# Extra products in TensorE's waits, and a later place for the stores of keys and values, in a cross-attention and coupling kernel

## The chip, the cores and the metric

The kernel runs on one core of a Trainium2 chip. The metric is the device time of one execution in microseconds (us). TensorE multiplies matrices (PE in the profile, PEld its weight loads), VectorE is DVE, ScalarE is ACT, GpSimd is POOL, and SyncE (SP) issues the DMAs.

## The reference

```python
x = x + xattn(layernorm(x), ctx)            # x 8 x 1024 x 512, ctx 8 x 64 x 512, 16 heads of 32
x = x + ffn(layernorm(x))

def xattn(q, kv):
    qh, kh = phase_sync(heads(q @ Wq.T + bq)), phase_sync(heads(kv @ Wk.T + bk))
    a = softmax(qh @ kh.T / sqrt(32))
    return merge(a @ heads(kv @ Wv.T + bv)) @ Wo.T + bo

def ffn(x):
    gf = global_net(x.mean(over the 1024 rows))          # three small layers
    out = x
    for _ in range(3):                                   # three cycles
        tf = sigmoid(gelu(gelu(gelu(out @ w1 + b1) @ w2 + b2) @ w3 + b3) @ w4 + b4)
        out = out + (0.1 + arange * (0.7 * gf + 0.3 * tf - 0.5) * 2) * twist(out)
    return out
```

## The kernel before

Each engine has one program, an ordered list of steps written out by hand, and semaphores between them. An engine never goes past a step whose wait is not over. There are eight batches of 1024 rows, each in two blocks (k) of 512 rows, and each block in four tiles of 128 rows (j or t). The attention of batch b runs interleaved with the coupling network of batch p = b - 1.

**Attention.** ScalarE normalizes a tile into PSUM and rounds it to f16 (`xh`, L764), VectorE makes the low half (`xl`, L1827), and SyncE issues a DMA transpose (`x_turn`, L3079) into `xoT`, or `x2T` for the second normalization. `xr` has two buffers, so `xh` of a tile waits until the transpose of the tile two before it has landed. `q` (L286) are 12 products of the query weights, `s` (L304) the scores of one tile (24 products into two PSUM banks), VectorE takes the maximum (L1839) and subtracts it (`sub`, L1847), ScalarE takes the exponential (L792), GpSimd normalizes, the probabilities are split (L804, L1869) and turned by DMA (`p_turn`, L3092). `pv` (L320) multiplies by the values, ScalarE and VectorE drain it (L815, L1874), and `wo` (L335, L337) is the output product of one tile, 13 products, drained by VectorE (L1881).

**Coupling network.** A batch has four units of 256 rows (k, h), dealt to three lanes of buffers, with a fourth lane for the last unit of all. `y` (L387) are 24 products of 256 columns into a lane's PSUM bank, drained by ScalarE (L837). `gz` (L344) are the global net's products; they wait for the column sums `gsum` (ScalarE, L776) of the whole batch. Each of three cycles of a unit goes `act1` (ScalarE, L850), rounding (VectorE, L1918) and low half (GpSimd, L2851), `l2` (L402, twice 12 products), `act2` (L858), `l3` (L414), `act3` (L866), `l4` (L422), and the coupling back on ScalarE (L877, L885), VectorE and GpSimd.

**Setup.** The keys and values of all batches are computed at the start into `kst` and `vst`. `kv_load(0)` takes batch 0's from there. `kv_store` (L3010, L3014) writes all of them to DRAM, and `kv_load(b)` of later batches reads them back from there; it and the first `y` of each lane wait for `kv_stored`. `load_next` (L3025) loads the next batch's x.

TensorE's bank numbers: `BANK_X` 0, scores `BANK_S` 1 and 2, `BANK_M` 3 and 4, lanes `BANK_F` 5, 6, 7 and 3.

Of the kernel before, what the change touches and what calls it, by code (L numbers as in the profile page):

```python
# [15 lines left out]
B, S, D = 8, 1024, 512  # L16
# [26 lines left out]
def cols(j):  # L43
    return slice(j * P, (j + 1) * P)


def program(nc, x, ctxT, wq, bq, wk, bk, wvT, bv, woT, bo, phase, cw1, cb1, cw2, cb2, cw3, cb3, cw4, cb4,
# [5 lines left out]
    with ExitStack() as ctx:  # L53
# [164 lines left out]
        def tensor_program(e):  # L218
# [53 lines left out]

            @staged
# [132 lines left out]
            @staged  # L406
            def l3(p, k, h, cy):
                L, u = unit(p, k, h)
                i = 3 * u + cy
                e.wait_ge(lg[L]["g2"], base(L, "g2") + 2 * i + 2)  # L410
                if u + cy == 0:
                    e.wait_ge(loaded["w3"], 16)
                for c in range(C2):
                    mm = e.matmul(ps[:, BANK_F[L], 0:LBLK], W3[:, c], zb[L][:, c], start=(c == 0), stop=(c == C2 - 1))  # L414
                mm.then_inc(lg[L]["l3"], 1)
# [17 lines left out]
            s(0, 0); s(0, 1); s(0, 2)  # L433
# [3 lines left out]
            s(0, 4); s(0, 5); s(0, 6)  # L437
            pv(0, 0, 0); pv(0, 0, 1)
            s(0, 7)
            wo(0, 0); wo(0, 1); wo(0, 2); wo(0, 3)  # L440
            pv(0, 1, 0); pv(0, 1, 1)
            wo(0, 4); wo(0, 5); wo(0, 6); wo(0, 7)
            y(0, 0, 1, 0); y(0, 0, 0, 0); y(0, 0, 1, 1); y(0, 1, 0, 0); y(0, 0, 1, 2); y(0, 1, 0, 1)
# [75 lines left out]
            for b, p in zip(range(2, 7), range(1, 6)):  # L519
# [60 lines left out]
                l2(p, 1, 1, 1, 0); l2(p, 1, 1, 1, 1)  # L580
                l3(p, 1, 1, 1)
                l4(p, 1, 1, 1)
# [65 lines left out]
            l2(6, 1, 1, 1, 0); l2(6, 1, 1, 1, 1)  # L648
            l3(6, 1, 1, 1)
            l4(6, 1, 1, 1)  # L650
# [35 lines left out]
            l2(7, 1, 0, 1, 0); l2(7, 1, 1, 0, 0); l2(7, 1, 1, 0, 1)  # L686
            l3(7, 1, 1, 0)
            l4(7, 1, 1, 0)
            l2(7, 1, 0, 1, 1)
            l3(7, 1, 0, 1)  # L690
            l4(7, 1, 0, 1)
            l2(7, 1, 1, 1, 0); l2(7, 1, 1, 1, 1)
            l3(7, 1, 1, 1)
            l4(7, 1, 1, 1)
            l2(7, 0, 1, 2, 0); l2(7, 0, 1, 2, 1); l2(7, 1, 0, 2, 0)
            l3(7, 0, 1, 2)
            l2(7, 1, 0, 2, 1)
            l4(7, 0, 1, 2)
            l3(7, 1, 0, 2)
            l4(7, 1, 0, 2)  # L700
            l2(7, 1, 1, 2, 0); l2(7, 1, 1, 2, 1)
            l3(7, 1, 1, 2)
            l4(7, 1, 1, 2)
# [2292 lines left out]
        def sync_program(e):  # L2996
# [140 lines left out]
            kv_store(0)  # L3137
# [4 lines left out]
            p_turn(0, 6, 0); p_turn(0, 7, 0); p_turn(0, 6, 1); p_turn(0, 7, 1)  # L3142
            load_next(0, 0)
# [158 lines left out]
```

## Time and profile before

| | |
|---|---|
| median of 3 runs | 1371.53 us (1369.87 to 1373.86) |
| the profiled execution's own time | 1371.05 us |
| its span, first to last instruction | 1369.0 us |
| mean granted TensorE clock over the span | 0.964 |
| PE busy | 1244.9 us (91%) |
| DVE, ACT, POOL busy | 1053.6, 1052.0 and 614.5 us |

The granted clock is the share of TensorE's full clock that it was given: 1.00 is 2.4 GHz, 0.50 is 1.2 GHz. The profile's own page cuts the span into 40 slices of 34.2 us.

### The profile page before, as it was taken

To read this page: it belongs to the slowest core of one execution; us is meant where nothing else is said; L and a number is where in the kernel's file an instruction comes from. 1 tells how busy PE (TensorE), PEld (TensorE's weight loads), DVE (VectorE), ACT (ScalarE), POOL (GpSimd) and SP (SyncE) were. 2 spreads that over 40 slices of the span, in tenths; PEclk is the share of its full clock that TensorE was granted. 3 is DMA by queue.
4 is the path that set the end of the run, shared out by engine and by line. 5 is a ranking of instruction groups with operands and counts; after the bars stand their busy time and mean duration, and the time that the engine had idled before them with its cause. 6 is when DMAs were issued, how large, how long until landed. Compare 5 with 4: busy or idle time off the path is not lost.

```text
span 1369.0 us, 27539 instructions
## 1 busy us (share of the span) xinstructions
PE 1244.9 (91%) x10264; PEld 868.0 (63%) x10264; DVE 1053.6 (77%) x2097; ACT 1052.0 (77%) x1886; POOL 614.5 (45%) x488
## 2 busy tenths in 40 slices
PE   7756899989999999999999999999999999988974
PEld 5322665658666776658666776658666776657863
DVE  4787459995889769985899669995899669994565
ACT  3444768888887978888887978888887877877655
POOL 0032025572455526562455526562455526462563
PEclk9967999999999999999999999999999999999997
DMA  7554423434254345433354335433354334431001
GB/s 246 156 88 108 91 49 72 93 70 98 53 119 80 71 78 93 102 71 93 71 108 79 77 71 93 102 70 93 72 107 78 81 75 78 78 52 42 32 1 62
DMA packets 323156, 114.81 MB, mean 84 GB/s; under 512 B 302416, under 2 KB 309456, under 8 KB 320848
## 3 DMA queue, kind: packets, MB, share of 16 engines
q1 hardware_dynamic: 323024, 113.06, 39.2%
q8 instruction: 81, 1.33, 0.4%
q14 instruction: 51, 0.42, 0.1%
HBM read 26.66 MB, written 18.87 MB: 33 GB/s over the span
## 4 chain that ended last, share of the span: by engine, by line
PE 60%; ACT 15%; DVE 11%; issue 6%; DMA 3%; POOL 2%; SPq 1%; ACTq 0%; DVEq 0%; POOLq 0%
PE ps L387 19%; PE ps L402 11%; PE ps L286 11%; PE ps L335 7%; ACT spent L776 4%; PE ps L414 3%; PE ps L304 2%; PE ps L422 2%; ACT z L850 2%; DMA x2T<-xr 2%; ACT z L858 2%; DVE xr L1827 2%; DVE z L1939 1%; DVE z L1927 1%; ACT xoT L815 1%
## 5 line engine op out<-in xcount | busy, mean ns | idle before, releaser
L2851 POOL TENSOR_TENSOR h<-z,h 128x512 f16<-128x512 f32 x186 | 234.6, 1271 | 385.5 <-DVE h L1918 385.5
L387 PE MATMUL ps<-x2T,W 128*128 128x256 f16 x3072 | 351.1, 273 | 6.6 <-ACT Y L837 4.0
L387 PEld LDWEIGHTS ps<-x2T,W 128*128 128x128 f16 x3072 | 297.4, 98 | 56.9 <-issue 8.8
L402 PE MATMUL ps<-h,W 128*128 128x256 f16 x2232 | 273.0, 280 | 6.4 <-POOL h L2851 6.2
L402 PEld LDWEIGHTS ps<-h,W 128*128 128x128 f16 x2232 | 221.7, 101 | 54.5 <-issue 13.7
L2844 POOL TENSOR_TENSOR prob<-prob,rc 128x512 f32<-128x512 f32 x128 | 140.1, 1117 | 104.2 <-DVE rc L1863 104.2
L335 PE MATMUL ps<-WO,xoT 128*128 128x512 f16 x768 | 180.1, 385 | 5.0 <-DVE xoT L1874 5.0
L286 PE MATMUL ps<-xoT,WQ 128*128 128x512 f16 x768 | 174.3, 380 | 0.7 <-issue 0.5
L1827 DVE TENSOR_TENSOR xr<-ps,xr 128x512 f16<-128x512 f32 x128 | 87.8, 686 | 82.9 <-ACT xr L764 82.6
L2860 POOL TENSOR_TENSOR z<-Y,coup 128x512 f32<-128x512 f32 x62 | 100.2, 1616 | 83.5 <-ACT coup L885 69.7
L850 ACT ACTIVATE z<-z,b_col 128x256 f32<-128x256 f32 x248 | 113.2, 500 | 30.7 <-DVE z L1939 30.6
L335 PEld LDWEIGHTS ps<-WO,xoT 128*128 128x128 f16 x768 | 75.4, 99 | 91.2 <-issue 7.2
L1918 DVE CAST h<-z 128x512 f16<-128x512 f32 x186 | 96.3, 531 | 46.4 <-ACT z L850 46.0
L286 PEld LDWEIGHTS ps<-xoT,WQ 128*128 128x128 f16 x768 | 74.5, 98 | 87.9 <-issue 4.6
L414 PE MATMUL ps<-z,W 128*128 128x256 f32 x372 | 100.7, 397 | 22.6 <-ACT z L858 21.8
L858 ACT ACTIVATE z<-ps,b_col 128x256 f32<-128x256 f32 x186 | 79.9, 470 | 49.1 <-PE ps L402 49.0
L2867 POOL TENSOR_TENSOR Y<-Y,coup 128x512 f32<-128x512 f32 x62 | 92.3, 1506 | 23.4 <-DVE coup L1951 23.4
L1939 DVE TENSOR_TENSOR z<-z,Y 128x512 f32<-128x512 f32 x124 | 97.4, 797 | 6.7 <-POOL Y L2867 4.9
L837 ACT ACTIVATE Y<-ps 128x512 f32<-128x512 f32 x124 | 71.6, 590 | 35.6 <-PE ps L387 35.3
L2837 POOL TENSOR_TENSOR rs<-ve,minus_half 128x4 f32<-128x4 f32 x32 | 35.6, 1113 | 131.0 <-DVE ve L1815 130.9
L414 PEld LDWEIGHTS ps<-z,W 128*128 128x128 f32 x372 | 65.5, 191 | 42.9 <-ACT z L858 32.7
L1839 DVE TENSOR_REDUCE mx<-ps 128x8 f32<-128x512 f32 x128 | 81.8, 673 | 12.1 <-PE ps L304 11.8
(159 smaller groups left out, 2064.2 us busy)
## 6 DMA issues: line engine op xcount, KB each, us to landing
xin<-x SPq DMA_DIRECT2D x16, 1024.0 KB, 5.5
out<-ot SPq DMA_DIRECT2D x64, 256.0 KB, 2.5
factor_rows<-coup SPq DMA_DIRECT2D x186, 0.5 KB, 2.1
pT<-pr SPq DMA_TRANSPOSE x128, 3.2
wq_s<-wq SPq DMA_DIRECT2D x1, 1024.0 KB, 5.9
wk_s<-wk SPq DMA_DIRECT2D x1, 1024.0 KB, 10.4
ctx_s<-ctxT SPq DMA_DIRECT2D x4, 256.0 KB, 10.3
wv_s<-wvT SPq DMA_DIRECT2D x1, 1024.0 KB, 10.9
```

The source lines that it names most:

```text
L286: mm = e.matmul(ps[:, bank], w, v, start=(n == 0), stop=(n == 3 * C - 1))
L335: e.matmul(ps[:, BANK_M + i % 2], w, v, start=(n == 0), stop=False)
L387: mm = e.matmul(ps[:, BANK_F[L], at * LBLK:(at + 1) * LBLK], w, v, start=(n == 0), stop=(n == 3 * C - 1))
L402: mm = e.matmul(ps[:, BANK_F[L], m * LBLK:(m + 1) * LBLK], w, v, start=(c + m + a == 0), stop=(c == C - 1 and m == C2 - 1 and a == 2))
L414: mm = e.matmul(ps[:, BANK_F[L], 0:LBLK], W3[:, c], zb[L][:, c], start=(c == 0), stop=(c == C2 - 1))
L850: e.activation(z[L][:, m], src, ACT.Gelu, bias=b1_col[:, m:m + 1]).then_inc(lg[L]["g1"], 1)
L858: e.activation(zb[L][:, m], src, ACT.Gelu, bias=b2_col[:, m:m + 1], scale=1.0 / WSCALE).then_inc(lg[L]["g2"], 1)
L1827: e.tensor_tensor(xr[:, n % 2, LO], ps[:, BANK_X], xr[:, n % 2, HI], ALU.subtract).then_inc(sg["xl"], 1)
L1939: e.tensor_tensor(z[L][:, pair(n)], z[L][:, pair(n)], Y[L][:, pair(n), 0], ALU.add).then_inc(lg[L]["pre"], 1)
L2844: e.tensor_tensor(part, part, wide(half_heads(rc[:, j], g)), ALU.mult).then_inc(sg["nrm"], 1)
L2851: e.tensor_tensor(h1[L][:, LO, pair(n)], z[L][:, pair(n)], h1[L][:, HI, pair(n)], ALU.subtract).then_inc(lg[L]["lo1"], 1)
L2860: e.tensor_tensor(z[L][:, pair(1)], Y[L][:, pair(1), 1], wide2(c1[L] if cy == 1 else b2[L]), ALU.mult).then_inc(lg[L]["mulg"], 1)
```

## The change

A helper `weight_products` issues n products of a part of the query weights with another part. Nothing reads their results. In batch 0 they go into lane 0's PSUM bank (`in_lane_bank`, once lane 2's), 512 columns each, 95 of them in twelve places. In each pass of batches p = 1 to 5 they go into the upper half of a lane's bank (`beside`), 256 columns each, 10 ahead of `l3(p, 1, 1, 1)` and 3 ahead of the `l4` behind it; in pass 6 it is 14 and 3. In the last batch they go into a score bank (`in_score_bank`), 512 columns each, 36 in fourteen places. Each group waits for a semaphore that frees its bank. `kv_store` moves from behind `x_turn(0, 0, 1, 0)` to behind the last `p_turn` of batch 0.

```diff
--- before.py
+++ after.py
@@ -270,6 +270,23 @@
                                   start=(c == 0), stop=(c == C - 1))
                 mm.then_inc(su["v_mul"], 1)
 
+            def weight_products(at, n):
+                for _ in range(n):
+                    e.matmul(at, WQ[:, HI, 0, cols(0)], WQ[:, HI, 1, 0:at.shape[-1]], start=True, stop=True)
+
+            def in_lane_bank(L, n):
+                e.wait_ge(su["v_lo"], B // 2)
+                weight_products(ps[:, BANK_F[L]], n)
+
+            def in_score_bank(n):
+                e.wait_ge(sg["sub"], 16 * B)
+                weight_products(ps[:, BANK_S], n)
+
+            def beside(p, k, h, cy, n):
+                L, u = unit(p, k, h)
+                e.wait_ge(lg[L]["g2"], base(L, "g2") + 2 * (3 * u + cy) + 2)
+                weight_products(ps[:, BANK_F[L], LBLK:BLK], n)
+
             @staged
             def q(b, k, m):
                 i = 24 * b + 4 * k + m
@@ -430,17 +447,36 @@
             q(0, 0, 0)
             vmul(0, 1); vmul(0, 2); vmul(0, 3)
             q(0, 0, 1); q(0, 0, 2); q(0, 0, 3)
-            s(0, 0); s(0, 1); s(0, 2)
+            in_lane_bank(0, 5)
+            s(0, 0)
+            in_lane_bank(0, 9)
+            s(0, 1)
+            in_lane_bank(0, 6)
+            s(0, 2)
             q(0, 1, 0)
             s(0, 3)
             q(0, 1, 1); q(0, 1, 2); q(0, 1, 3)
-            s(0, 4); s(0, 5); s(0, 6)
-            pv(0, 0, 0); pv(0, 0, 1)
+            in_lane_bank(0, 5)
+            s(0, 4)
+            in_lane_bank(0, 14)
+            s(0, 5)
+            in_lane_bank(0, 9)
+            s(0, 6)
+            pv(0, 0, 0)
+            in_lane_bank(0, 13)
+            pv(0, 0, 1)
             s(0, 7)
+            in_lane_bank(0, 8)
             wo(0, 0); wo(0, 1); wo(0, 2); wo(0, 3)
-            pv(0, 1, 0); pv(0, 1, 1)
+            in_lane_bank(0, 2)
+            pv(0, 1, 0)
+            in_lane_bank(0, 8)
+            pv(0, 1, 1)
+            in_lane_bank(0, 8)
             wo(0, 4); wo(0, 5); wo(0, 6); wo(0, 7)
-            y(0, 0, 1, 0); y(0, 0, 0, 0); y(0, 0, 1, 1); y(0, 1, 0, 0); y(0, 0, 1, 2); y(0, 1, 0, 1)
+            y(0, 0, 1, 0); y(0, 0, 0, 0)
+            in_lane_bank(2, 8)
+            y(0, 0, 1, 1); y(0, 1, 0, 0); y(0, 0, 1, 2); y(0, 1, 0, 1)
             gz(0, 0)
             y(0, 0, 0, 1); y(0, 1, 0, 2)
             gz(0, 1)
@@ -578,7 +614,9 @@
                 l4(p, 1, 0, 1)
                 wo(b, 6); wo(b, 7)
                 l2(p, 1, 1, 1, 0); l2(p, 1, 1, 1, 1)
+                beside(p, 1, 0, 1, 10)
                 l3(p, 1, 1, 1)
+                beside(p, 1, 0, 1, 3)
                 l4(p, 1, 1, 1)
                 l2(p, 0, 1, 2, 0); l2(p, 0, 1, 2, 1); l2(p, 1, 0, 2, 0); l2(p, 1, 0, 2, 1)
                 l3(p, 0, 1, 2); l3(p, 1, 0, 2)
@@ -646,7 +684,9 @@
             l4(6, 1, 0, 1)
             wo(7, 6); wo(7, 7)
             l2(6, 1, 1, 1, 0); l2(6, 1, 1, 1, 1)
+            beside(6, 1, 0, 1, 14)
             l3(6, 1, 1, 1)
+            beside(6, 1, 0, 1, 3)
             l4(6, 1, 1, 1)
             l2(6, 0, 1, 2, 0); l2(6, 0, 1, 2, 1); l2(6, 1, 0, 2, 0); l2(6, 1, 0, 2, 1)
             l3(6, 0, 1, 2); l3(6, 1, 0, 2)
@@ -684,22 +724,37 @@
             y(7, 1, 1, 3)
             l4(7, 0, 1, 1)
             l2(7, 1, 0, 1, 0); l2(7, 1, 1, 0, 0); l2(7, 1, 1, 0, 1)
+            in_score_bank(3)
             l3(7, 1, 1, 0)
+            in_score_bank(1)
             l4(7, 1, 1, 0)
             l2(7, 1, 0, 1, 1)
+            in_score_bank(3)
             l3(7, 1, 0, 1)
+            in_score_bank(3)
             l4(7, 1, 0, 1)
+            in_score_bank(5)
             l2(7, 1, 1, 1, 0); l2(7, 1, 1, 1, 1)
+            in_score_bank(3)
             l3(7, 1, 1, 1)
+            in_score_bank(1)
             l4(7, 1, 1, 1)
-            l2(7, 0, 1, 2, 0); l2(7, 0, 1, 2, 1); l2(7, 1, 0, 2, 0)
+            in_score_bank(2)
+            l2(7, 0, 1, 2, 0)
+            in_score_bank(2)
+            l2(7, 0, 1, 2, 1); l2(7, 1, 0, 2, 0)
             l3(7, 0, 1, 2)
             l2(7, 1, 0, 2, 1)
             l4(7, 0, 1, 2)
+            in_score_bank(6)
             l3(7, 1, 0, 2)
+            in_score_bank(1)
             l4(7, 1, 0, 2)
+            in_score_bank(2)
             l2(7, 1, 1, 2, 0); l2(7, 1, 1, 2, 1)
+            in_score_bank(3)
             l3(7, 1, 1, 2)
+            in_score_bank(1)
             l4(7, 1, 1, 2)
 
         def scalar_program(e):
@@ -3134,12 +3189,12 @@
             load_late(0, 0); load_late(0, 2); load_late(0, 3); load_late(0, 1)
             kv_load(0)
             x_turn(0, 0, 1, 0)
-            kv_store(0)
             x_turn(0, 0, 1, 1); x_turn(0, 0, 1, 2); x_turn(0, 0, 1, 3)
             load_late(0, 4)
             p_turn(0, 0, 0); p_turn(0, 1, 0); p_turn(0, 0, 1); p_turn(0, 1, 1); p_turn(0, 2, 0); p_turn(0, 2, 1)
             p_turn(0, 3, 0); p_turn(0, 3, 1); p_turn(0, 4, 0); p_turn(0, 4, 1); p_turn(0, 5, 0); p_turn(0, 5, 1)
             p_turn(0, 6, 0); p_turn(0, 7, 0); p_turn(0, 6, 1); p_turn(0, 7, 1)
+            kv_store(0)
             load_next(0, 0)
             x_turn(0, 1, 0, 0); x_turn(0, 1, 0, 1); x_turn(0, 1, 0, 2); x_turn(0, 1, 0, 3)
             kv_load(1)
```

TensorE's order where batch 0's scores begin. Before (L286 is `q`, L304 `s`, L320 `pv`):

```order
L286 MATMUL ps<-xoT,WQ 128x512 x36
L304 MATMUL ps<-kblocks,qT 128x128 x72
L286 MATMUL ps<-xoT,WQ 128x512 x12
L304 MATMUL ps<-kblocks,qT 128x128 x24
L286 MATMUL ps<-xoT,WQ 128x512 x36
L304 MATMUL ps<-kblocks,qT 128x128 x72
L320 MATMUL ps<-pT,vblocks 32x512 x48
L304 MATMUL ps<-kblocks,qT 128x128 x24
```

The changed kernel has the same steps (L303 is `q`, L321 `s`), and L275 are the extra products; `ps<-WQ` is all that they name:

```order
L303 MATMUL ps<-xoT,WQ 128x512 x36
L275 MATMUL ps<-WQ 128x512 x5
L321 MATMUL ps<-kblocks,qT 128x128 x24
L275 MATMUL ps<-WQ 128x512 x9
L321 MATMUL ps<-kblocks,qT 128x128 x24
L275 MATMUL ps<-WQ 128x512 x6
L321 MATMUL ps<-kblocks,qT 128x128 x24
L303 MATMUL ps<-xoT,WQ 128x512 x12
L321 MATMUL ps<-kblocks,qT 128x128 x24
L303 MATMUL ps<-xoT,WQ 128x512 x36
L275 MATMUL ps<-WQ 128x512 x5
L321 MATMUL ps<-kblocks,qT 128x128 x24
```

The 72 products of three tiles of scores, which stood together, now have 9 and 6 extra products between them and 5 ahead, and so on in the next three.

SyncE's order in batch 0, from the loads of keys and values. Before (L3010 and L3014 are `kv_store`, L3079 `x_turn`, L3092 `p_turn`, L3025 `load_next`):

```order
L3042 DMA kblocks<-kst 32x2x256 x4
L3079 DMA_TRANSPOSE xoT<-xr 128x8x128
L3010 DMA k_blocks<-kst 128x4096
L3014 DMA v_blocks<-vst 64x8x256 x4
L3079 DMA_TRANSPOSE xoT<-xr 128x8x128 x3
L3001 DMA b_col<-cb 128x4
L3001 DMA b_col<-cb 128x2
L3001 DMA b_col<-cb 128x1
L3001 DMA gb_col<-gb 128x2
L3001 DMA gb_col<-gb 128x1
L3092 DMA_TRANSPOSE pT<-pr 128x8x128 x16
L3025 DMA xin<-x 128x2048
```

After (L3134 is `x_turn`, L3147 `p_turn`, L3065 and L3069 `kv_store`, L3080 `load_next`):

```order
L3097 DMA kblocks<-kst 32x2x256 x4
L3134 DMA_TRANSPOSE xoT<-xr 128x8x128 x4
L3056 DMA b_col<-cb 128x4
L3056 DMA b_col<-cb 128x2
L3056 DMA b_col<-cb 128x1
L3056 DMA gb_col<-gb 128x2
L3056 DMA gb_col<-gb 128x1
L3147 DMA_TRANSPOSE pT<-pr 128x8x128 x16
L3065 DMA k_blocks<-kst 128x4096
L3069 DMA v_blocks<-vst 64x8x256 x4
L3080 DMA xin<-x 128x2048
L3134 DMA_TRANSPOSE x2T<-xr 128x8x128 x4
```

The five stores went past three transposes of x, five small loads and 16 transposes of probabilities. They now stand ahead of the next batch's load and of the four transposes into `x2T`.

TensorE's order at the end of a pass (p = 2). Before (L402 is `l2`, L414 `l3`, L422 `l4`):

```order
L402 MATMUL ps<-h,W 128x256 x24
L414 MATMUL ps<-z,W 128x256 x2
L422 MATMUL ps<-z,W 128x256
L402 MATMUL ps<-h,W 128x256 x48
L414 MATMUL ps<-z,W 128x256 x4
```

After (L419 is `l2`, L431 `l3`, L439 `l4`; the trace shows twice as many records for the f32 products as stand here):

```order
L419 MATMUL ps<-h,W 128x256 x24
L275 MATMUL ps<-WQ 128x256 x10
L431 MATMUL ps<-z,W 128x256 x2
L275 MATMUL ps<-WQ 128x256 x3
L439 MATMUL ps<-z,W 128x256
L419 MATMUL ps<-h,W 128x256 x48
L431 MATMUL ps<-z,W 128x256 x4
```

The 10 and the 3 extra products stand ahead of `l3` and ahead of `l4`; the 48 products of four `l2` behind them did not move.

## Rows read from the trace of the kernel before

**Rows 1.** The page: granted clock by slice, and the ending chain by engine.

```profile
PEclk9967999999999999999999999999999999999997
...
PE 60%; ACT 15%; DVE 11%; issue 6%; DMA 3%; POOL 2%; SPq 1%; ACTq 0%; DVEq 0%; POOLq 0%
```

**Rows 2.** Busy time by stretch, then granted clock, DMA share, GB/s.

```profile
60.00:145.00 85.00, 52.22 (x442) 24.88 (x443) 63.21 (x104) 35.55 (x46) 19.15 (x17) 0.76 0.55 115
...
449.97:456.80 6.83, 6.16 (x27) 4.18 (x27) 5.63 (x9) 6.40 (x13) 6.11 (x6) 0.50 0.20 39
```

**Rows 3.** The chain that ended last, 56 to 160 us: start, length.

```profile
66.30 5.45 DMA xoT<-xr
...
95.14 1.48 PE ps L304 x24
...
105.81 1.53 PE ps L320 x18
...
110.94 4.23 PE ps L335 x12
...
131.28 5.05 PE ps L335 x12
```

**Rows 4.** The timeline, 60 to 73 us: start, length, [idle <-releaser].

```profile
60.66 5.54 SPq L3014 DMA_DIRECT2D v_blocks<-vst  x4
...
64.90 1.29 DVE L1839 TENSOR_REDUCE mx<-ps 128x8 f32<-128x512 f32 x2 [0.27 <-PE ps L304]
...
72.46 0.69 DVE L1827 TENSOR_TENSOR xr<-ps,xr 128x512 f16<-128x512 f32 x1 [6.27 <-ACT xr L764]
```

**Rows 5.** DMA issues, 38 to 140 us: count, median us to landing.

```profile
x2T<-xr SPq DMA_TRANSPOSE x4, 3.1
```

**Rows 6.** TensorE's waits, 58 to 155 us: total, times, longest.

```profile
PE ps L304 <- DVE prob L1847: 18.6, 4, 9.5
PE ps L320 <- DVE xoT L1874: 6.2, 2, 3.8
PE ps L335 <- DVE xoT L1874: 4.5, 2, 2.3
PE ps L304 <- DVE qT L1832: 3.4, 2, 1.7
PE ps L387 <- ACT Y L837: 2.2, 1, 2.2
```

**Rows 7.** The timeline, TensorE's groups while the granted clock was 1.00.

```profile
90.38 0.84 PE L304 MATMUL ps<-kblocks,qT 64*128 64x128 f16 x24 [1.71 <-DVE qT L1832]
...
121.04 2.75 PE L335 MATMUL ps<-WO,xoT 128*128 128x512 f16 x12
...
128.18 0.84 PE L320 MATMUL ps<-pT,vblocks 64*32 64x512 f16 x24 [2.45 <-DVE xoT L1874]
...
444.23 2.78 PE L402 MATMUL ps<-h,W 128*128 128x256 f16 x24
```

**Rows 8.** The timeline of ScalarE, 142 to 160 us.

```profile
142.33 1.06 ACT L776 ACTIVATE spent<-x2T 128x1024 f16<-128x1024 f16 x1 [3.92 <-DMA x2T<-xr]
...
148.22 0.78 ACT L755 ACTIVATE ps<-xin,nm,rs 128x512 f32<-128x512 f32 x1 [1.19 <-DVE nm L1821]
...
159.52 0.60 ACT L837 ACTIVATE Y<-ps 128x512 f32<-128x512 f32 x1 [0.81 <-PE ps L387]
```

**Rows 9.** The timeline, 448 to 461 us: TensorE, VectorE and ScalarE.

```profile
448.89 1.13 PE L414 MATMUL ps<-z,W 128*128 128x256 f32 x4 [1.87 <-ACT z L858]
...
451.70 7.89 PE L402 MATMUL ps<-h,W 128*128 128x256 f16 x48
...
458.38 0.67 DVE L1827 TENSOR_TENSOR xr<-ps,xr 128x512 f16<-128x512 f32 x1
...
459.63 0.84 ACT L858 ACTIVATE z<-ps,b_col 128x256 f32<-128x256 f32 x2 [1.78 <-PE ps L402]
```

**Rows 10.** The timeline of TensorE in the last products.

```profile
1348.53 4.01 PE L402 MATMUL ps<-pT,W 128*128 128x256 f16 x24 [0.64 <-POOL pT L2851]
```

## The prediction

> **What bounds the kernel now.** I read the page first. The chain that ended last lies on PE for 60%, and the granted clock is full in all but the third and fourth slice and, slightly, at the ends [rows 1]. So TensorE is the bound from about 145 us on, and the start is something else. The stretches say what: from 60 to 145 us PE is busy for 52 of 85 us at a mean clock of 0.76, while VectorE is busy for 63 [rows 2]. The chain there passes from engine to engine, and where it is on PE its pieces are long: a `wo` of 12 products takes 4.23 and 5.05 us [rows 3], where the same 12 take 2.75 at full clock [rows 7]. In each later pass one low stretch is left, as 449.97 to 456.80 us at exactly 0.50 [rows 2]. It falls behind a wait of 1.87 us ahead of `l3`, and holds most of the 48 products of four `l2`, which take 7.89 us [rows 9] against twice 2.78 for 24 at full clock [rows 7].
>
> **The stores, moved.** SP issues the five stores ahead of the transpose of the sixth tile; the four of the values alone occupy it for 5.54 us [rows 4], and that transpose then takes 5.45 us from issue to landing among their data [rows 3]. Such transposes take 3.1 us in the median elsewhere in this stretch [rows 5]. ScalarE cannot round the eighth tile until that landing, VectorE waits for ScalarE, and behind this wait in VectorE's order stand the subtraction of the second tile of scores and all that follows. Without the stores the transpose is issued at about 60.1, where the stores began, and lands by 63.3. The next thing VectorE is late for is its own maximum, which ends at 66.19 (64.90 + 1.29), and the step that began at 72.46 can follow at once: its idle time was 6.27 us [rows 4]. I take **-6.3**. The next tile's transpose leaves earlier by the same amount, so TensorE's second `q` does too.
>
> What the stores cost in the new place: they go out behind the last transpose of probabilities, with nothing to wait for, and SP has about 9 us before the first transpose into `x2T` is ready; their issue takes some 6 and the load of x behind them less than 1. So the issue is hidden. The data are not quite: 2 MB of stores and 1 MB of x are in flight when that transpose goes. Right behind the stores a transpose took 5.45 instead of 3.1 us, which bounds the price at 2.3; zero is the other end. ScalarE has no slack there, since it waited 3.92 us for the last of these transposes [rows 8]. The last store is about 4 us old instead of new, so I take **+1.5**.
>
> **The extra products in batch 0.** 12 products of 512 columns take 2.75 us at full clock [rows 7], 0.23 each. 93 of the 95 lie in waits that sum to 34.9 us [rows 6], of which 6.3 go with the stores: 28.6 us of waiting against 21.4 of products. The largest group but one, 13, takes 3.0 us in a wait of 3.8 [rows 6]. At full clock each group ends before its wait does, so they cost nothing; what hides them is VectorE's softmax.
>
> Their effect is that TensorE's idle stretches shrink to under 1 us in most places, so the clock that the profile shows at 0.50 for most of this stretch should stay at 1.00. On the chain this is worth, up to the first normalization of the second kind: scores 1.48 to 0.84, **-0.6**; `pv` 1.53 to 0.84 or 0.89, **-0.6**; the first `wo` 4.23 to 2.75, **-1.4** [rows 3, 7]. The rest of the chain is VectorE's and does not change. With the stores that makes 8.9. The second group of `wo`, 5.05 to 2.75, would give 2.3 more, but the transposes into `x2T`, on which ScalarE's column sums wait, start ahead of it and move by 8.9 only. ScalarE then goes from the sums to the next normalization, where it had 1.19 us of slack [rows 8]; so I count **-1.2** of the 2.3. The `y` products after the eighth group of 8 also ran partly at 0.50; ScalarE was idle for them for 0.81 us [rows 8], so **-0.8**. Start: -6.3 - 2.6 - 1.2 - 0.8 + 1.5 = **-9.4**.
>
> **The passes.** 24 products of 256 columns take 2.78 us [rows 7], 0.116 each: 10 take 1.2 us of the 1.87 us wait, 3 take 0.35 us ahead of `l4`. They cost nothing while ScalarE is busy with the column sums, which it is for all of that wait. If the clock stays up, the 48 `l2` products need 5.6 instead of 7.9 us. But not all 2.3 us are passed on. ScalarE waited only 1.78 us for them, and the normalization right behind its `act2` needs VectorE's low half, which ends at 459.05 (458.38 + 0.67) [rows 9], where it began at about 460.4 (behind 459.63 + 0.84). This limits the gain to **-1.3** for a pass; what is late next is VectorE, with its coupling work. The transposes, the sums and `gz` behind it all move by 1.3, and from there TensorE is the bound again. Five passes show this low stretch at the same place, each of 6.8 us: **-6.5**. In the sixth (pass 6) the low stretch is 3.4 us, and the chain there runs over a transpose of 5.1 us, so I count nothing.
>
> **The last batch.** 36 products of 0.23 us stand in waits of 0.6 to 1.8 us, in groups of 1 to 6; they fit. Two low stretches lie there. Only the last one is on the chain: 24 products in 4.01 us [rows 10] against 2.78, **-1.2**. The other delays a unit whose result waits in ScalarE's order anyway.
>
> **The sum.** Against the profiled execution's 1371.05 us, which is 0.5 below the median: 1371.05 - 9.4 - 6.5 - 1.2 = 1353.95, so 1354.
>
> **Rivals.**
> *The clock falls all the same* (0.19). Products of 64 rows or 32 columns, f32 products and waits of 0.3 to 1 us stay between the extra ones, and a pass that is shorter by 1 us puts its waits at another moment each time, as it does to the longer waits of batch 1's start, behind which nothing fell before. Then the passes give nothing: 1371.05 - 10.6 = 1360.
> The Trainium skill ("TensorE: Matmul & The Clock Gate", A second HAM failure mode) says that frequent micro-idles between groups of products make the clock oscillate; by that rule the products bring little where short waits remain, and the time would be this 1360. The trace agrees only in part: from 300 to 1150 us it shows many short waits and a fall at one of them alone in each pass.
>
> *The stores collide with the transposes* (0.08). If the transposes into `x2T` queue behind all of the stores' and the load's data, each of the first two is late by up to 2.3 us and the loss of the start is given back: the gain of 6.3 shrinks to about 0, 1371.05 - 17.1 + 6.3 = 1360.
>
> *More is passed on* (0.10). VectorE's order behind the passes' `l2` is not as rigid as I read it, all 2.3 us pass, and the stores cost nothing: 1354 - 5 x 1.0 - 1.5 = 1347.5.
>
> *The extra products overrun* (0.03), the case on the other side. Should the clock stay at 0.50 in batch 0, as it did for much of it, a product takes 5.05 / 12 = 0.42 us [rows 3], and 93 take 39 us in 28.6 us of waits: at least 10.4 us are added to the chain. In the passes 10 take 2.1 us in 1.87, some 0.3 for each, and in the last batch about 3 more. With the stores' 4.8 gained: 1371.05 + 10.4 + 1.5 + 3 - 4.8 = 1381. It decides once more than about half of batch 0's groups run at the low clock. The profile speaks against it: where PE is busy without a break the clock comes back, in the passes after 6.83 us [rows 2], and the first groups start while it is still at 1.00.
>
> **How the numbers follow.** My forecast has 0.60: 1349 to 1359, with the collision's bounds (0 to 2.3) and 0.5 to 1.5 for each pass. With the first two rivals at 1360 the range has to reach up, with the third down: 1346 to 1363. It leaves out the overrun and mixtures of the first two. A measurement of this kernel tells 0.3%, 4.1 us, from no change. Faster is every case but the overrun and a coincidence of clock and collision: 0.93; within 0.3% 0.04; slower 0.03.
>
> **What would show it.** VectorE's idle of 6.27 us at the eighth tile gone, and the second `q` 6 us earlier; granted clock near 1.00 from 60 to 145 us, with `wo` groups of 2.75; `y` of batch 0 beginning some 9 to 10 us earlier; passes of about 152.4 us from `l3` to `l3` instead of 153.8, with 48 `l2` products in under 6; the last 24 in 2.8. I would be wrong if `x2T`'s transposes land late, if `l3` or `l4` starts behind an extra product instead of behind ScalarE, or if the low stretch only moves.

## The result, and the profile after

The changed kernel takes 1366.18 us (median of 7 runs, 1363.12 to 1369.19); the kernel before, run beside it, 1371.53 (7 runs, 1368.99 to 1374.48). The ratio is 0.996 with a 95% interval of 0.9944 to 0.9975: faster, by 5.35 us, where 17 were forecast. The time lies outside the range. The profiled execution took 1366.63 us against 1371.05, 4.4 less; that is the difference which the traces can be asked about.

The page of the kernel after: TensorE's busy time, its granted clock by slice, and the chain that ended last, by engine.

```profile
PE 1267.1 (93%) x10477; PEld 877.7 (64%) x10477; DVE 1051.8 (77%) x2097; ACT 1050.1 (77%) x1886; POOL 614.6 (45%) x488
...
PEclk9989999999999999999999999999999999999998
...
PE 57%; ACT 16%; DVE 14%; issue 7%; DMA 3%; POOL 3%; SPq 1%; ACTq 0%; DVEq 0%; POOLq 0%
```

The 6 and the 7 of [rows 1] are gone, and the mean clock rose from 0.964 to 0.989. Read by the clock alone the change did what it should. The stretches of [rows 2], asked again (busy time by stretch, then granted clock, DMA share, GB/s):

```profile
60.00:145.00 85.00, 68.06 (x535) 30.94 (x534) 65.00 (x106) 37.00 (x49) 19.14 (x17) 0.94 0.62 115
...
450.00:457.00 7.00, 5.94 (x41) 4.26 (x42) 5.88 (x8) 6.60 (x15) 6.64 (x6) 1.00 0.20 37
```

So the time is to be looked for elsewhere. I set the same group of TensorE against itself in both traces, and noted by how much it comes earlier:

| place on TensorE | before, us | after, us | earlier by |
|---|---|---|---|
| second `q`, (0,1,0) | 76.37 | 71.55 | 4.8 |
| first `wo` starts | 110.94 | 106.60 | 4.3 |
| first `wo` ends | 115.17 | 109.35 | 5.8 |
| first transpose into `x2T` issued (SP) | 132.41 | 127.61 | 4.8 |
| `gz(0)` | 166.25 | 164.77 | 1.5 |
| `gz(1)`, pass 0 between them | 315.99 | 318.40 | -2.4 |
| `gz(7)`, passes 1 to 6 between them | 1245.29 | 1241.78 | 3.5 |
| end of the span | 1369.0 | 1364.6 | 4.4 |

Four sums stand in it: the start gave 1.5 us (forecast 9.4), pass 0 took 3.9 (forecast nothing), passes 1 to 6 gave 5.9 (forecast 6.5), the last batch 0.9 (forecast 1.2). A pass is here the way from `gz(0)` of one batch to that of the next.

**Where the start went.** TensorE's waits from 58 to 155 us, as in [rows 6]: what is waited for, total, times, longest.

```profile
PE ps L321 <- DVE prob L1902: 4.9, 4, 3.0
PE ps L352 <- DVE xin L1936: 4.5, 2, 4.3
PE ps L337 <- DVE xoT L1929: 2.6, 2, 2.1
PE ps L352 <- DVE xoT L1929: 1.8, 2, 1.4
PE ps L337 <- DMA pT<-pr: 1.4, 1, 1.4
```

The waits for `prob` and `xoT` shrank, filled by products and shortened by the stores' departure. Two are new: `wo` waits 4.3 us for VectorE's `xin`, and `pv` 1.4 us for a transpose of probabilities. SP's timeline there: start, length.

```profile
118.29 0.53 SPq L3065 DMA_DIRECT2D k_blocks<-kst  x1
118.87 5.67 SPq L3069 DMA_DIRECT2D v_blocks<-vst  x4
124.58 1.31 SPq L3080 DMA_DIRECT2D xin<-x  x1
```

And the chain of the same stretch: start, length, what.

```profile
116.17 3.94 DMA pT<-pr
...
120.19 0.89 PE ps L337 x24
...
127.61 6.87 DMA x2T<-xr
...
134.56 0.61 ACT xr L819
...
135.19 0.69 DVE xr L1882
135.88 0.61 DVE xin L1936
...
136.53 4.45 PE ps L352 x12
```

The transpose issued at 127.61, 3.0 us behind the issue of the load, lands after 6.87 us; [rows 5] have 3.1. ScalarE needs its landing to overwrite `xr`, VectorE's low half stands behind ScalarE, `xin` stands behind that in VectorE's order, and the third `wo` needs `xin`. TensorE is idle for 4.27 us, the granted clock falls to 0.50 (from 137.4 to 140.8 us), and 12 products take 4.45 us, not 2.75.

**The passes.** The stretch of [rows 9] in the kernel after, TensorE: start, length, count, [idle before it].

```profile
448.15 1.26 PE L275 MATMUL ps<-WQ 128*128 128x256 f16 x10
450.17 1.13 PE L431 MATMUL ps<-z,W 128*128 128x256 f32 x4 [0.76 <-ACT z L913]
451.13 0.49 PE L275 MATMUL ps<-WQ 128*128 128x256 f16 x3
...
452.96 3.04 PE L419 MATMUL ps<-h,W 128*128 128x256 f16 x24 [0.30 <-POOL h L2906]
456.16 2.78 PE L419 MATMUL ps<-h,W 128*128 128x256 f16 x24 [0.16 <-POOL h L2906]
```

`l3` still starts behind ScalarE, not behind an extra product; the 48 products take 5.8 us, not 7.89, and no low stretch is left in passes 1 to 6. In pass 0, which has no extra products, two have appeared that the kernel before did not show. The first of them, in the kernel before and, below the dots, in the kernel after:

```profile
227.18 1.13 PE L414 MATMUL ps<-z,W 128*128 128x256 f32 x4 [1.74 <-ACT z L858]
228.88 0.70 PE L422 MATMUL ps<-z,W 128*128 128x256 f32 x2 [0.57 <-ACT z L866]
229.41 1.03 PE L414 MATMUL ps<-z,W 128*128 128x256 f32 x4
...
227.97 1.13 PE L431 MATMUL ps<-z,W 128*128 128x256 f32 x4 [1.73 <-ACT z L913]
229.67 1.22 PE L439 MATMUL ps<-z,W 128*128 128x256 f32 x2 [0.56 <-ACT z L921]
230.68 1.91 PE L431 MATMUL ps<-z,W 128*128 128x256 f32 x4
```

The second group of four f32 products takes 1.03 us before and 1.91 after: the clock stood at 0.66 in the mean from 229 to 234 us, and it fell again from 297.8 to 301.2. The wait ahead of the first group is the same in both, 1.74 and 1.73 us; only behind the second of them does the clock fall.

### The profile page after: what moved, and what is told of

The parts are those of the page before. It is cut to its first block, busy times and chain, and to the rows that moved or that the text cites. A ratio compares the mean times of both kernels' runs of the same rounds, so it can differ in the third digit from the quotient of the medians.

```text
span 1364.6 us, 27965 instructions
## 1 busy us (share of the span) xinstructions
PE 1267.1 (93%) x10477; PEld 877.7 (64%) x10477; DVE 1051.8 (77%) x2097; ACT 1050.1 (77%) x1886; POOL 614.6 (45%) x488
## 4 chain that ended last, share of the span: by engine, by line
PE 57%; ACT 16%; DVE 14%; issue 7%; DMA 3%; POOL 3%; SPq 1%; ACTq 0%; DVEq 0%; POOLq 0%
PE ps L404 19%; PE ps L303 12%; PE ps L419 9%; PE ps L352 6%; ACT spent L831 4%; PE ps L431 3%; PE ps L321 2%; DVE xr L1882 2%; DMA x2T<-xr 2%; ACT xr L819 2%; ACT z L905 2%; ACT ps L810 2%; PE ps L439 2%; DVE z L1994 1%; ACT z L913 1%
## 5 line engine op out<-in xcount | busy, mean ns | idle before, releaser
L404 PEld LDWEIGHTS ps<-x2T,W 128*128 128x128 f16 x3072 | 296.2, 98 | 55.9 <-issue 9.9
L419 PE MATMUL ps<-h,W 128*128 128x256 f16 x2232 | 265.8, 274 | 9.0 <-POOL h L2906 8.1
L419 PEld LDWEIGHTS ps<-h,W 128*128 128x128 f16 x2232 | 215.8, 98 | 55.4 <-issue 19.7
L303 PE MATMUL ps<-xoT,WQ 128*128 128x512 f16 x768 | 175.5, 382 | 4.7 <-issue 4.6
L303 PEld LDWEIGHTS ps<-xoT,WQ 128*128 128x128 f16 x768 | 74.7, 98 | 93.1 <-issue 10.8
L431 PE MATMUL ps<-z,W 128*128 128x256 f32 x372 | 99.0, 394 | 13.6 <-ACT z L913 12.6
L1894 DVE TENSOR_REDUCE mx<-ps 128x8 f32<-128x512 f32 x128 | 81.9, 673 | 15.6 <-PE ps L321 15.3
L431 PEld LDWEIGHTS ps<-z,W 128*128 128x128 f32 x372 | 65.8, 191 | 33.9 <-ACT z L913 23.4
```

The costliest lines, as they stand in the source:

```text
L303: mm = e.matmul(ps[:, bank], w, v, start=(n == 0), stop=(n == 3 * C - 1))
L404: mm = e.matmul(ps[:, BANK_F[L], at * LBLK:(at + 1) * LBLK], w, v, start=(n == 0), stop=(n == 3 * C - 1))
L419: mm = e.matmul(ps[:, BANK_F[L], m * LBLK:(m + 1) * LBLK], w, v, start=(c + m + a == 0), stop=(c == C - 1 and m == C2 - 1 and a == 2))
```

## The experiments

Each ran beside the kernel before on its own chip, and the ratio is to that; medians of different chips are compared by their ratios only. "Alone" means on the kernel before. My theory ahead of them: the stores' new place makes the transposes into `x2T` late, and this, with what follows in pass 0, is where the gain went. The main rival: the clock falls somewhere else as soon as one fall is filled, so that products in general bring little.

**1. The stores in the change's place, alone** (`e1_store_alone`).

```diff
             x_turn(0, 0, 1, 0)
-            kv_store(0)
...
             p_turn(0, 6, 0); p_turn(0, 7, 0); p_turn(0, 6, 1); p_turn(0, 7, 1)
+            kv_store(0)
```

> The kernel before with the five stores moved to their new place and no extra product. Theory A (the stores collide with the transposes into x2T in the new place): VectorE's wait of 6.3 us at the eighth tile is gone, some 5 us are gained by 80 us, and one of the four first transposes into x2T takes over 5 us and gives 2 to 4 us of it back; the sums' product gz of batch 0 stands 1 to 3 us earlier than before, time 1368 to 1371. Theory B (the extra products, not the stores, ate the gain): all four transposes land in 3 to 4 us, gz stands 5 to 6 us earlier, time 1365 to 1366.5.

Measured: 1369.37 us against 1373.29, ratio 0.9971 (0.9948 to 0.9993). It gained 4.9 us at the third tile of scores (69.54 against 74.40) and kept 2.3 of them at `gz(0)` (164.00). The first transpose into `x2T` left 5.4 us behind the load here and took 4.66 us. The numbers are those of theory A, but the loss is not where it puts it: of the 2.6 us, 2.4 are gone before that transpose is issued (129.91 against 132.41), because the second `q` took 4.76 us at the low clock instead of 3.49, and the first `wo` 5.28 instead of 4.23. The way from that issue to `gz(0)` is only 0.25 us longer than before (34.09 against 33.84): without the products the late landing cost next to nothing.

**2. All products of the change, stores in the old place** (`e2_products_alone`): the change without the piece of experiment 1.

> The changed kernel with the stores back at their old place, so the extra products alone. Theory A: the transposes into x2T take 3.1 us again; the first wo groups run in 2.75 us, gz of batch 0 stands 3 to 5 us earlier than in the kernel before, the passes are as in the changed kernel, time 1362 to 1366, no slower than the changed kernel. Theory B: gz of batch 0 no earlier than before or later, time 1369 to 1373.

Measured: 1367.48 us, ratio 0.9964 (0.9946 to 0.9982). The transposes into `x2T` are on time (3.12 us), TensorE waits for `xin` at most 0.5 us ahead of a `wo`, and the groups of `wo` take 2.76. Yet the first transpose into `x2T` is issued at 132.07, only 0.3 us earlier than before, and `gz(0)` comes 2.2 earlier.

**3. The stores ahead of the transposes of probabilities** (`e3_store_ahead_of_p_turns`), the rest as in the change.

```diff
             load_late(0, 4)
+            kv_store(0)
             p_turn(0, 0, 0); p_turn(0, 1, 0); p_turn(0, 0, 1); p_turn(0, 1, 1); p_turn(0, 2, 0); p_turn(0, 2, 1)
...
-            kv_store(0)
             load_next(0, 0)
```

> The changed kernel with the five stores behind the small loads and ahead of the 16 transposes of probabilities, at about 72 us, where the DMA engines are little used. Theory A: the transposes into x2T take 3.1 us, VectorE no longer waits 5.4 us at 135 us, gz of batch 0 5 to 6 us earlier than in the changed kernel (less 1 to 2 if the first p_turns are late), time 1360 to 1363. Theory B: no more than 1 us from the changed kernel's 1366.

Measured: 1361.55 us, ratio 0.9919 (0.9895 to 0.9942), which just clears the change's 0.9944 to 0.9975. `gz(0)` at 158.39 instead of 164.77. The stores are issued from 71.97 to 77.84, where no transpose is due, and the chain has

```profile
126.38 3.11 DMA x2T<-xr
```

But pass 0 took 155.51 us, with three low stretches (160.6 to 164.0, 222.0 to 228.8, 293.7 to 297.1).

**4. The change without its 82 products in the passes** (`e4_no_pass_products`): the four `beside` calls taken out.

> The changed kernel without the 82 products in the passes p = 1 to 6. If they are worth 1.3 us in each of five passes, as forecast, the distance from gz of batch 1 to gz of batch 7 grows by 6 to 7 us against the changed kernel and the time is 1371 to 1373. If they are worth nothing (the low stretch only moved), both are as in the changed kernel.

Measured: 1379.29 us, ratio 1.0057 (1.0037 to 1.0076): slower than the kernel before by 0.6%. Its profiled run is its fastest (1370.29) and has low stretches in four passes (2, 3, 5 and 6); the other runs show mean clocks of 0.976 to 0.983, where the profiled one has 0.987. From `gz(1)` to `gz(7)` it takes 933.3 us, 9.9 more than the kernel after, where 6 to 7 were expected, and 4.0 more than the kernel before. The low clock is not all of it: pass 4 has no low stretch and takes 155.98 us against 152.97, with two waits on "issue", of 1.80 and 0.85 us, that the kernel after does not have there. For the start this kernel is a repetition of the changed one, with the same code up to there. Its stores are issued from 115.20, and the chain again has

```profile
124.42 6.32 DMA x2T<-xr
```

**5. The 82 products alone** (`e6_pass_products_alone`).

> The kernel before with the 82 products of the passes p = 1 to 6 and nothing else. If a pass gains the forecast 1.3 us by the clock, the five passes are 152.4 us long and the time is 1365 to 1367, 6 to 7 under the kernel before. If the 13 us by which the kernel without them was slower than the changed one are their worth wherever they stand, it is 1359 to 1361. If their worth comes only with the changed start (by the moment at which the clock is decided), it is 1370 to 1373.

Measured: 1368.39 us, ratio 0.9968 (0.9951 to 0.9985), 4 to 5 us, which lies between the expectations of 1365 to 1367 and 1370 to 1373. Passes 1 to 6 sum to 925.5 us against 929.3.

**6. Products in pass 0 too** (`e5_pass0_products`): experiment 3 with 33 more, which leave out nothing and whose result nobody reads. `in_scores(b, n)` is `in_score_bank(n)` with a wait for batch b.

```diff
+            in_scores(1, 6)
             gz(0, 0)
+            in_scores(1, 2)
             y(0, 0, 0, 1); y(0, 1, 0, 2)
             gz(0, 1)
...
+            beside(0, 0, 0, 1, 12)
             l3(0, 1, 0, 0)
+            beside(0, 0, 0, 1, 3)
             l4(0, 1, 0, 0)
...
+            beside(0, 1, 0, 1, 7)
             l3(0, 1, 1, 1)
+            beside(0, 1, 0, 1, 3)
             l4(0, 1, 1, 1)
```

> The stores ahead of the p_turns, as in e3, and 33 more extra products where the clock fell in pass 0 of e3: 6 ahead of the first gz and 2 behind it, 12 and 3 ahead of l3 and l4 of unit (0, 1, 0, 0), 7 and 3 ahead of l3 and l4 of unit (0, 1, 1, 1). Theory C (falls behind waits that stayed unfilled take back part of the start's gain): no stretch at 0.50 between 150 and 300 us, from gz of batch 0 to gz of batch 1 150 to 152 us instead of 155.5, time 1357 to 1360. Against it (these falls are hidden by other engines): the distance stays at 154 or more and the time within 1 us of e3's.

Measured: 1359.03 us, ratio 0.9906 (0.9881 to 0.9931). Pass 0 fell from 155.51 to 152.2 us. TensorE at the `l3` whose wait was 1.73 us in the kernel after:

```profile
218.72 1.48 PE L275 MATMUL ps<-WQ 128*128 128x256 f16 x12
220.53 1.13 PE L435 MATMUL ps<-z,W 128*128 128x256 f32 x4 [0.33 <-ACT z L923]
221.50 0.49 PE L275 MATMUL ps<-WQ 128*128 128x256 f16 x3
222.23 0.70 PE L443 MATMUL ps<-z,W 128*128 128x256 f32 x2 [0.24 <-ACT z L931]
222.76 1.03 PE L435 MATMUL ps<-z,W 128*128 128x256 f32 x4
```

Where experiment 3 and the change show 1.9 us for the second group of `l3`, it is 1.03 here. Two cautions. The ratio is not to be told from experiment 3's. And experiment 8, the same code as experiment 3 up to the last batch, shows 1.03 at this place too, behind its unfilled wait of 1.73 us, and takes 153.73 us for pass 0: the gain of the fillings there is 1.5 to 3.3 us, by which trace it is set against. One low stretch is left in pass 0, from 300.5 to 303.9 us.

**7. Experiment 3 without the 95 products of batch 0** (`e7_no_batch0_products`).

> The changed kernel with the stores ahead of the p_turns (e3) and without the 95 products of batch 0. By the forecast's terms these were worth 0.6 + 0.6 + 1.4 us up to the first normalization of the second kind and 1 to 2 us behind it: gz of batch 0 stands 3 to 5 us later than in e3 and the time is 1364 to 1367. If VectorE hides the slow products, gz stands within 1 us of e3's and the time within 1.5 us.

Measured: 1362.40 us, ratio 0.993 (0.9903 to 0.9957), not to be told from experiment 3. `gz(0)` is 4.1 us later (162.52), pass 0 is 4.3 shorter (151.25), and `gz(1)` is the same (313.77 against 313.90). In these two traces pass 0 takes back all that the products gave in batch 0. In experiment 8, with experiment 3's code up to there, `gz(1)` comes at 312.23, and 1.5 us are left.

**8. Experiment 3 without the 36 products of the last batch** (`e8_no_last_products`).

> The changed kernel with the stores ahead of the p_turns (e3) and without the 36 products of the last batch. By the forecast's term they are worth 1.2 us: 24 products in 4.0 instead of 2.8 us at the end, time 1362 to 1364. Rival: they are worth nothing, or cost, since the groups of 5 and 6 end behind their waits: time 1360 to 1362.

Measured: 1362.94 us, ratio 0.9941 (0.9916 to 0.9965). From `gz(7)` to the end it takes 121.67 us, and experiment 3 takes 121.67 as well: in the trace these products are worth nothing, and the medians don't resolve it.

**9. The stores in the better place, alone** (`e9_store_ahead_alone`): the kernel before with experiment 3's move, no product added.

> The kernel before with one change: the five stores go out on SP behind the last early load of weights and ahead of the transposes of probabilities, instead of ahead of the transpose of the sixth tile. No product is added. My theory (the new place costs only because the transposes into x2T land late behind the stores; the move ahead of the probabilities' transposes keeps the early gain without that cost): gz(0) comes 6 to 7 us earlier than in the kernel before (it was 2.3 earlier with the stores in the place of the change), and the median is 4 to 7 us below the kernel before: 1365 to 1368. Rival (the extra products are what makes the better place pay, since a wait that ends earlier is filled by products at the low clock): gz(0) only 3 to 4 us earlier and the median 2 to 4 us below, 1369 to 1371.

Measured: 1365.40 us against 1372.19, ratio 0.9958 (0.9937 to 0.998). One moved line gives 6.8 us, as much as the whole change. `gz(0)` came 5.9 earlier, just under the 6 to 7 expected.

**10. Seven products more near 297 us** (`e10_gap_at_297`), on experiment 6.

```diff
-            l3(0, 0, 1, 2); l3(0, 1, 0, 2)
+            l3(0, 0, 1, 2)
+            beside(0, 1, 1, 1, 7)
+            l3(0, 1, 0, 2)
```

> The best version so far (stores ahead of the probabilities' transposes, all products of the change, 33 more in pass 0) with 7 more products of 256 columns between l3(0,0,1,2) and l3(0,1,0,2), where its trace shows TensorE idle for 2.89 us behind a transpose that took 4.76 us, and the clock fall behind it. Theory (each fall of the clock follows a single wait that nothing fills): no low stretch at 297 to 304 and pass 1 about 153 us instead of 155.7, median 1 to 3 us below that version. Rival (the late transpose is what cost the pass, and it falls elsewhere in another build): pass 1 near 153 whether or not a low stretch stands there, and the median within 1 us of that version, 1358 to 1360.

Measured: 1358.86 us, ratio 0.9903 (0.9873 to 0.9934), the fastest here and not to be told from experiment 6. The wait stayed, less the time of the products in it, and the low stretch that followed it is gone:

```profile
296.94 0.93 PE L275 MATMUL ps<-WQ 128*128 128x256 f16 x7
299.76 1.13 PE L435 MATMUL ps<-z,W 128*128 128x256 f32 x4 [1.89 <-ACT z L925]
301.02 0.70 PE L443 MATMUL ps<-z,W 128*128 128x256 f32 x2
```

In experiment 6 that wait was 2.89 us, and the four products of `l4` behind it took 2.08; here they take twice 0.70. Pass 1 is 153.07 us, against 155.66. This is not shown to come from the filling: `gz(1)` is no earlier than in experiment 6 (311.41 against 311.05), and the low stretch there ended at 303.9, ahead of it. In experiment 11 the wait at this place was 1.01 us without a filling, no low stretch followed, and pass 1 took 154.27.

**11. Experiment 6 without the 82 products of the passes** (`e11_e5_without_passes`), which asks experiment 4's question again.

> The same best version without the 82 products ahead of l3 and l4 of passes 1 to 6; those of pass 0, of batch 0 and of the last batch stay. It asks again what the pass products are worth: alone on the kernel before they gave 4.8 us, and taking them from the changed kernel cost 13. Theory A (they are worth the filled waits, about 1 us for each of six passes): median 5 to 7 us above that version, 1364 to 1366, with the low stretches of the kernel before back at l3 of most passes. Theory B (together with the other products they are worth more, since a fall in one pass moves others into place): 10 us or more, 1369 and up.

Measured: 1361.42 us, ratio 0.9922 (0.9898 to 0.9946), 2.6 us above experiment 10 on the same chip; passes 1 to 6 sum to 926.3 us against 922.6. Experiment 10 has the seven products near 297 us besides; against experiment 6, from which nothing else differs, the ratios are 2.2 us apart with overlapping intervals, and passes 1 to 6 sum to the same (926.3 and 926.6), since pass 1 ran long there. The low stretches are back in passes 3, 4, 5 and 6. Theory B is out, and A was too high: 2.2 to 2.6 us by the medians, nothing to 3.7 by the traces.

## Why the prediction was wrong

The kernels side by side. The third column is the way from the first transpose into `x2T` to `gz(0)`, which leaves out what happened ahead of it; the last is how long the granted clock stood at 0.50 in pass 0.

| kernel | `x2T` issued | to `gz(0)` | pass 0 | at 0.50 in pass 0 |
|---|---|---|---|---|
| before | 132.41 | 33.84 | 149.74 | 0 |
| 9, stores better, no products | 125.89 | 34.43 | 151.06 | 6.8 |
| 7, the same for the start | 128.68 | 33.84 | 151.25 | 3.4 |
| 1, stores as in the change, no products | 129.91 | 34.09 | 153.78 | 6.8 |
| 2, products, stores not moved | 132.07 | 32.03 | 153.62 | 3.4 |
| after | 127.61 | 37.16 | 153.63 | 6.8 |
| 4, the same for the start | 124.42 | 35.24 | 153.60 | 3.4 |
| 3, products, stores better | 126.38 | 32.01 | 155.51 | 13.6 |
| 8, the same for the start | 126.47 | 32.03 | 153.73 | 3.4 |
| 6, and products in pass 0 | 126.80 | 32.05 | 152.20 | 3.4 |
| 10, the same | 127.36 | 32.01 | 152.04 | 0 |
| 11, the same | 125.48 | 31.99 | 152.14 | 0 |

The forecast was 17.1 us, the traces show 4.4. Of the 12.7 that are missing, 7.9 are missing in the start, 3.9 went in pass 0, and 0.9 in the rest. The start's 7.9 divide into 3.6 for the stores' new place, 4.1 up to the issue of the first transpose into `x2T` (4.8 instead of 8.9), and 0.2.

**The failed step: "the last store is about 4 us old instead of new, so I take +1.5".** It cost 5.1 us in the kernel after (37.16 - 32.0) and 3.2 in experiment 4. I bounded the price at 2.3 by one transpose of the kernel before that went out right behind the stores. That bound was taken from the wrong quantity. The landing is fixed by the data ahead of it, not by the moment of the issue: 15.6 us behind the first store of values in the kernel after (118.87 to 134.48), 15.0 in experiment 4 (115.78 to 130.74), 15.6 in experiment 1 (119.00 to 134.57), though the three transposes left 3.0, 3.1 and 5.4 us behind the load. The DMA engines were busy all that time:

```profile
118.87:134.48 15.61, 11.13 (x90) 4.45 (x90) 6.69 (x15) 5.96 (x9) 1.01 (x1) 1.00 1.05 245
```

So a transpose that wants to land sooner waits for the 2 MB of stores and the 1 MB of x ahead of it; in the old place the stores alone were ahead. As an estimate: 3.15 MB at this stretch's 245 GB/s are 12.8 us, and with the usual 3.1 of a transpose that makes 134.2, from the first store at 118.29; it landed at 134.48. The same sum for the old place, 2.1 MB at 240 GB/s from 60.09, gives 71.9 against 71.75. The sooner the transpose is issued behind the stores, the more it pays: 6.87 and 6.32 us when it came 8.7 and 8.6 us behind the first store of values (after and experiment 4), 4.66 when it came 10.9 behind (experiment 1). Of the 5.1 us, 3.8 are the landing (6.87 - 3.1), and the fall of the clock behind TensorE's wait adds 1.7 on `wo` (4.45 - 2.75), less what slack there was. Experiment 4 has the late landing without the fall, and pays 3.2. That the stores' place is the cause is shown by experiments 2 and 3, in which nothing but that differs and no such delay stands; the traces give 5.1 us, the ratios of experiment 3 and the change (0.9919 and 0.996) 0.41%, 5.6 us. The rival "the stores collide", at 1360, named the mechanism, with the same wrong cap.

**The second: "on the chain this is worth, up to the first normalization", 2.6 us for scores, `pv` and the first `wo`.** Experiment 2 has it at 0.3: `x2T`'s first transpose at 132.07 against 132.41. Measured from the second `q`, so without what the stores did ahead of it, the way to that issue is 54.8 to 57.0 us in the eight traces with the products (mean 55.9) and 55.7 to 58.4 in the five without (mean 56.8). That is 0.8 us in the mean, in ranges that overlap. In experiment 2 the parts can be told. The second `q` itself runs at the low clock, 4.90 us instead of 3.49, and this costs 1.4. The scores and `pv` give 0.8, where 1.2 were forecast. The first `wo` gives 1.4 as forecast, and 1.2 of it end in the new wait for `pT` (1.57 us; 1.38 in the kernel after, where that transpose takes 3.94). What is late next behind a shortened step was named for the stores, and not for this, and that the low clock would come to another group was not reckoned with.

The other half of the products' worth in batch 0 was read rightly: the last `wo` groups and `y` were to give 1.2 + 0.8, and the column shows 33.84 - 32.0 = 1.8.

**-6.3 for the stores' departure** came out at 4.8 at the second `q`, or 5.4 without the first loads, 0.6 us later in this execution. The transpose was issued at 59.33, where about 60.1 was forecast, but landed after 5.36 us (3.1 assumed), one of the slow transposes of the last section:

```profile
59.33 5.36 DMA xoT<-xr
...
69.57 1.46 PE ps L321 x19
...
71.55 4.68 PE ps L303 x11
```

VectorE's 6.27 us of idle time is gone. That `q` still runs mostly at the low clock (4.90 us for its 12 products, which take 2.75 at full clock), and more of it than before (3.49).

**The omission: pass 0.** The sum begins the passes' gain with five passes and holds pass 0 for unchanged. Its waits ahead of `l3` have no extra products, and the profiled execution of before had shown no fall there, which I took for a property of the place. The table says otherwise: pass 0 takes 149.7 us before, 151.1 to 151.3 in experiments 7, 9 and 5 (151.22), and 153.6 to 155.5 in the five kernels with batch 0's products and none in pass 0; experiment 1, without products, takes 153.8 all the same.

The fall is only a part of it. In the kernel after, the lead of 1.5 us at `gz(0)` becomes a lag of 2.4 in four pieces: 1.4 at 180 us, where TensorE waits 1.20 us on "issue" for a transpose that takes 4.8; 0.9 at 210 us, where it waits 0.77 for one of 4.6; 1.5 behind the first fall; 0.1 behind the second, whose slower products are hidden.

```profile
209.93 2.75 PE L303 MATMUL ps<-xoT,WQ 128*128 128x512 f16 x12 [0.77 <-issue]
```

So 2.3 of the 3.9 us are late transposes, and 1.6 the clock. With products in pass 0 too it takes 152.0 to 152.2, and in experiments 10 and 11, where no low stretch is left in it, it is still 2.3 longer than before. That the fillings bring pass 0 down from 153.6 and more is shown in three traces against five; what else makes it longer than before is shown for the kernel after only. Nor is it shown that the clock falls more where batch 0 ran at full clock: the last column has 3.4 to 13.6 us for the five with the products, and 0 to 6.8 for the kernel before and experiments 9, 7, 1 and 5 (6.8).

The rival "the clock falls all the same" had this mechanism, but put it in the later passes, where nothing fell. The Trainium skill ("TensorE: Matmul & The Clock Gate", A second HAM failure mode) speaks of frequent micro-idles that make the clock oscillate. The traces agree only in part. Waits of 0.2 to 0.8 us stay in every pass of the kernel after, and single ones of 1.0 to 1.85 us in passes 2, 4 and 6, and passes 1 to 6 have no fall. Falls stand behind single waits of 2.89 and 4.27 us, but the one at 297.8 us in the kernel after stands behind waits of 1.04 and 0.56. And the wait of 1.73 or 1.74 us ahead of pass 0's `l3` is there in ten traces (before, after, and experiments 1 to 5 and 7 to 9), and the clock falls behind it in two, the kernel after and experiment 3. What decides between them the runs do not show.

**The passes, -6.5**, came out at 5.9 in the trace. By the medians these products are worth 4 to 5 us alone, and 2.6 on top of everything else, and 13 in experiment 4. The mechanism is right (`l2` 5.8 us, the clock at 1.00); in passes 3 to 5 of the two traces it gave 1.0 to 1.2 us each, and by the medians, but for experiment 4, 0.4 to 0.8 for each of six passes, where 1.3 for each of five was forecast. That the trace's sum comes so near is in part luck: pass 2 was 0.6 longer than before, with a wait of 1.85 us on "issue", and passes 1 and 6 gave 1.7 each, of which 1.3 and nothing were forecast. **The last batch, -1.2**, gave 0.9 in the trace, of which experiment 8 gives the products nothing: the last 24 products take 2.98 us, not 4.01, but the chain there has other waits.

**What stays open.** Experiment 4 is slower than the kernel before by 7 us, and than the change by 13; experiments 5 and 11 speak for 2 to 5. Its profiled run, its fastest, shows 9.9 us in passes 1 to 6, partly low clock and partly waits on "issue"; what made its other runs slower still is not shown, only that they had lower clocks. Single traces scatter at the same place with the same code: 3 us at the first transpose into `x2T` (experiments 7 and 9; the kernel after and 4), and 5.1 us at `gz(0)` (164.77 in the kernel after, 159.66 in experiment 4). So the start gave 1.5 us in one execution of this code and 6.6 in another, and a difference of that size between two traces is no finding unless a chain shows it.

## What to carry to other kernels

Price a transfer behind others in the same queue by the bytes ahead of it over the rate of the stretch, and not by how late another transfer was once; then look for a place where nothing is due before that time is over, since the better place alone (experiment 9) was worth about as much here as 213 extra products (experiment 2). When waits are filled in one stage, look at the waits of the next stage too, although its trace shows no fall yet: the same wait of 1.7 us had a fall behind it in some executions here and none in others. And for each microsecond removed from TensorE name the wait that ends next, for each term and not only for the large one.

## What the runs showed of the hardware

Transposes that usually land in 3.1 us take 4.3 to 5 now and then, and TensorE then waits 0.8 to 1.9 us with "issue" as the releaser. In the kernel after, the DMA queues from 175 to 181 us:

```profile
q8 instruction: 1, 0.02, 1.0%
issues: line engine op xcount, KB each, median us to landing
xoT<-xr SPq DMA_TRANSPOSE x1, 4.8
```

and TensorE behind it:

```profile
180.31 2.75 PE L303 MATMUL ps<-xoT,WQ 128*128 128x512 f16 x12 [1.20 <-issue]
```

The queue q8, "instruction", moves 83 packets of 16 KB in the whole execution. In the kernel after, 23 of the 256 transposes take over 4.3 us, and while 18 of them are in flight one of these packets starts; of the 191 that land within 3.3 us it is 9. In the kernel before it is 16 of 20, and 17 of 187. Most of the others over 4.3 us are issued behind large loads or stores. No run took the fetches away, so this is a coincidence in time and not a shown cause. Which transposes it meets changes with every inserted instruction, and so do the microseconds. This may be part of why two builds differ by some us where their code is the same. The Trainium skill ("Runtime: NRT & Kernel Launch", Instruction fetch mechanics) calls the cost of fetching the next block of instructions mostly hidden. That the packets hold up an engine directly, no trace here shows; beside it stand the 1.7 us by which such a transpose lands later (4.8 against 3.1).
